# Taking a gate increment out of SP's stream in three gather passes of a four-layer graph network

## The reference

```
# layer 0: messages from source rows and 3 edge features, summed at the destination
tmp = relu(concat(h[src], edge_attr) @ W1.T + b1)
hN  = segment_sum(tmp, dst);  y = relu(concat(h, hN) @ W2.T);  x += y / norm(y)
# layer 1: eight relations
xt  = einsum('ni,rio->rno', h, weight)
x  += relu(segment_sum(xt[edge_type, dst], src) + bias)
# layer 2: attention with 8 heads, softmax over the edges of a destination, batch norm
# layer 3: gcn
x  += leaky(segment_sum(w[:, None] * h[dst], src) @ W + b)
```

## Time and profile before

| what | value |
|---|---|
| median of three runs | 7142.75 us |
| the three runs | 7142.75, 7143.59, 7132.6 us |
| profiled execution, span of the page | 7126.6 us |
| profiled execution, another time than the span | none on the page |
| busy in the span | PE 60%, POOL 54%, DVE 47%, PEld 38%, ACT 20% |
| DMA | 541.25 MB, mean 76 GB/s |
| mean granted clock of PE | 0.676 of full speed |

### The profile page before, as it was taken

The page is one execution under the profiler, slowest core; times in us unless marked ns, Lnnn a source line. Parts: engine busy times, 40 slices in busy tenths (PEclk is TensorE's granted clock), DMA queues, the critical chain, the costliest instruction groups (busy, mean ns, idle before and its releaser), DMA issues. The chain is left out here.

```text
span 7126.6 us, 113087 instructions
## 1 busy us (share of the span) xinstructions
PE 4263.3 (60%) x13279; PEld 2710.9 (38%) x13284; DVE 3340.4 (47%) x11588; ACT 1440.5 (20%) x4442; POOL 3826.6 (54%) x4006
## 2 busy tenths in 40 slices
PE   4324666667724434966665665777777764656665
PEld 1202333333313211434343334555566553434443
DVE  5124555666502101345555555555555564444444
ACT  0202333333312100100000002444444440000000
POOL 3465555555562574036666665555555525666665
PEclk7655766666656656976667676777766766776677
DMA  1112333333300101434444443333333324444443
GB/s 45 40 30 58 80 80 81 80 78 78 73 6 1 32 21 49 147 107 98 98 98 97 97 98 77 82 80 82 82 81 81 81 62 94 95 94 95 94 94 87
DMA packets 1059254, 541.25 MB, mean 76 GB/s; under 512 B 864525, under 2 KB 956238, under 8 KB 1058889
## 3 DMA queue, kind: packets, MB, share of 16 engines
q0 software_dynamic: 177920, 424.21, 21.2%
q1 hardware_dynamic: 507624, 90.64, 6.8%
q10 hardware_dynamic: 373600, 25.30, 3.3%
HBM read 449.78 MB, written 89.82 MB: 76 GB/s over the span
## 5 line engine op out<-in xcount | busy, mean ns | idle before, releaser
L1727 PE MATMUL psS_plain_src<-got_plain_src,hot_plain_src 128*128 x3328 | 1374.7, 561 | 982.0 <-SPq L1558 559.6
L1727 PEld LDWEIGHTS psS_plain_src<-got_plain_src,hot_plain_src 128*128 128x128 f32 x3328 | 828.0, 273 | 1477.6 <-issue 1356.1
L685 POOL DMA_INDIRECT got_attend_dst<-dram_gtab,recs_attend_dst x832 | 812.2, 976 | 643.3 <-DVE msg_attend_dst L766 300.1
L1601 DVE TENSOR_TENSOR sums<-sums,psS_plain_src 128x257 f32 x1664 | 700.8, 421 | 901.6 <-issue 412.4
L1576 POOL DMA_INDIRECT got_edge_mlp_dst<-dram_ptab,rows_i_edge_mlp_dst x784 | 741.8, 946 | 595.4 <-SPq L1555 402.1
L561 POOL DMA_INDIRECT dram_rec_src<-rec_src x784 | 765.7, 977 | 508.3 <-issue 245.4
L1576 POOL DMA_INDIRECT got_plain_src<-dram_xtab,rows_i_plain_src x784 | 746.7, 952 | 478.3 <-SPq L1555 292.1
L1576 POOL DMA_INDIRECT got_plain_src<-dram_htab,rows_i_plain_src x784 | 746.7, 952 | 456.0 <-SPq L1555 268.6
L1738 PE MATMUL psS_edge_mlp_dst<-msg_edge_mlp_dst,hot_edge_mlp_dst 128*128 128x256 f32 x1664 | 792.2, 607 | 173.2 <-DVE sage_sums L1601 89.0
L880 PE MATMUL psS_attend_dst<-msg_attend_dst,hot_attend_dst 128*128 128x264 f32 x1664 | 757.2, 549 | 41.1 <-issue 32.0
L1948 PE MATMUL psO_tab<-w_tab,hT_tab 128*128 128x512 f32 (+1 forms) x980 | 476.8, 636 | 348.7 <-DVE out_tab L1924 190.9
(11 more groups left out here) (366 smaller groups left out, 4563.9 us busy)
## 6 DMA issues: line engine op xcount, KB each, us to landing
dram_xtab<-out_tab SPq DMA_DIRECT2D x48, 1024.0 KB
recs_plain_src<-dram_rec_src ACTq DMA_DIRECT2D x1664, 4.0 KB
recs_edge_mlp_dst<-dram_rec_dst ACTq DMA_DIRECT2D x832, 4.0 KB
recs_attend_dst<-dram_rec_dst SPq DMA_DIRECT2D x832, 4.0 KB
got_attend_dst<-dram_gtab,recs_attend_dst POOLq DMA_INDIRECT x832
dram_rec_src<-rec_src POOLq DMA_INDIRECT x784
got_edge_mlp_dst<-dram_ptab,rows_i_edge_mlp_dst POOLq DMA_INDIRECT x784
got_plain_src<-dram_xtab,rows_i_plain_src POOLq DMA_INDIRECT x784
```

The lines of the kernel that those rows point to most:

```text
L685: nc.gpsimd.indirect_dma_start(got[:, u, 0:w], None, table, bass.IndirectOffsetOnAxis(rec_i[:, u, index_word:index_word + 1], 0)).then_inc ...
L1601: nc.vector.tensor_tensor(here, here, psS[t[1] % banks][:, 0:cols], ALU.add).then_inc(added, 1)
L1727: nc.tensor.matmul(psS[t[1] % banks][:, 0:cols], hot[:, t[1], :], flat[:, bass.ds(slots.of(u), cols)], start=True, stop=True).then_inc(sum ...
```

## The change

The two lines of the gate go out of SP's program in `pair_pass`: its construction, and the step between the wait for used pairs and the raise of `free`. Other gates of the kernel, on SP in `edge_pass`, on DVE and on POOL, stay.

```diff
         @block.sync
         def _(sp):
-            gate = Gate(sp, c.passed["sp"])
             pairs_of = Places(nc.sync, (done, 0), tiles, U, sh.NT, least=1)
...
                     sp.wait_ge(used, pairs_of.of(u))
-                    gate.step()
                     sp.sem_inc(free, 1)
                 if (t := tiles.at(i, u, AHEAD)) is not None:
                     sp.wait_ge(row_in[t[1]], 16 * (t[0] + 1))
                     sp.sem_inc(landed, 1)
```

## The result

The kernel became slower: 7168.27 us (median of 8 runs, 7160.27 to 7185.72) against 7142.86 (8 runs, 7132.6 to 7159.09), a ratio of 1.0041 with a 95% interval of 1.0031 to 1.0051. The 25 us are on the other side of "no change" from the forecast of 150 us gained, and the time lies above the range.

A forecast was written before the change was run, and what follows sets the result against it. SP's instruction stream was taken to bound passes B and C. Gains of 142 us there and 8 us in pass A made 150 us, from the 7142.75 us median to 6993 us; range 6880 to 7150.

The forecast's parts named there:

- no change: Rival, chance 0.09: SP keeps four instructions a tile, or 0.71 us pieces come by the clock; time 7143 us.
- In B and C SP's instruction stream itself is what sets the pace: Plain passes on dram_xtab (B) and dram_htab (C): SP waits for practically nothing, yet POOL waits for SP.
- 221 to 243 us of waiting for L1555: POOL's real waiting before gathers, 243 us in pass B and 221 in C, nearly all for SP's raise of free.
- The price: What one removed SP instruction saves: 0.067 us at the fast pace, 0.61 us at the slow one.
- a count of 13 pieces for 16 instructions: Slow stretch of pass C: 16 SP instructions in 9.8 us, so fewer instructions should need fewer 0.71 us pieces.
- The cycle: Passes B and C: SP crawls during gathers, sprints when POOL lacks slots; one instruction less means fewer pauses.
- The 189 us: Gain in passes B and C from fewer POOL pauses: 99 us in B and 90 us in C.
- the 142 taken: Three quarters of the 189 us gain in passes B and C; the quarter off was a choice.
- Small gain: Rival, chance 0.20: SP relieved, but PE or ACT's record loads take over; gain 20 to 100 us, time 7043 to 7123.
- Pass A: The edge_mlp pass, 612 to 1947 us: only the step from used to free gets shorter, gain 8 us.
- if the cover fails (ACT made slower by closer gathers), pass A loses: Rival "slower", chance 0.15: closer gathers in the edge_mlp pass shrink ACT's good time; time about 7205 us.
- 65 us as the price: Slower rival's loss in the edge_mlp pass: 10% more of ACT's 651 us of unexplained idle.

The follow-up runs named there:

- e3: Kernel before with a second gate increment behind the first in all three passes; ratio 0.9952, 7016.34 us against 7049.93.
- e2: Kernel before with the gate taken out of pass A alone; ratio 1.0030, pass A 1339.0 us.
- e1: Kernel before with the gate taken out of passes B and C, kept in pass A; ratio 1.0014, pass A 1327.1 us.
- e12: Separate small program: 160 semaphore increments on SP, alone, beside 24 POOL gathers, beside ACT loads and more; 0.24 us an instruction beside gathers.
- e14: Kernel before, pass A without the gate, POOL blanking a small tile and waiting for it ahead of each gather; ratio 1.0018, pass A 1353.8 us.
- e10: Kernel before with three gates in pass A, ahead of the wait for used; B and C keep one; ratio 0.9890, 6973.47 us.
- e8: Kernel before with three gates in pass A, between the wait for used and the raise of free; ratio 0.9891, pass A 1268.3 us.
- e11: Kernel before, pass A without the gate but with three more SP register instructions a tile ahead of the wait; ratio 0.9883, 6973.64 us.
- e4: Kernel before with its one gate moved behind the raise of free; ratio 1.0015, pass A 1330.6 us.
- e9: Kernel before without the gate in any of the three passes, one more SP register record a tile ahead of the wait; ratio 1.0018.
- e13: Kernel before, pass A without SP's gate but with three increments per pair on PE's queue; ratio 1.0060, pass A 1370.5 us.
- e15: Kernel before with five gates in pass A, ahead of the wait for used; ratio 0.9934, pass A 1291.6 us.
- e5: Kernel before, gate kept, DVE adding only 32 of 257 columns in pass C; ratio 0.9987, pass C 1205.6 us.
- e6: Kernel before without the gate in any pass, DVE adding only 32 of 257 columns in pass C; ratio 1.0043, pass C 1196.4 us.

## Why the prediction was wrong

The step that failed is "In B and C SP's instruction stream itself is what sets the pace". It rested on SP's absent waits together with POOL's 221 to 243 us of waiting for L1555. Two gates in B and C should then have cost about as much as one was to give; they cost 28 us in both against one (e3 against e2) and 16 against none at all (e3 against e1), and taking one away made B 6 us longer and C 6 us shorter. The instruction did have a price on SP: the 313.5 us of new wait over 1536 instructions are an estimate of 0.20 us each. The passes gave none of it back. The reading that fits is that SP was nearly always late by about as much as used was late. A queue that is held up for 0.71 us at a time, and then comes to a wait already met, shows no wait, whether or not the wait would have lasted as long: absence of waits showed that SP had no slack, not that its slack was worth anything. After the change the 313.5 us of wait appeared at once.

**The price.** The two paces of SP, 0.067 and 0.61 us, are real (e12: 0.061 alone, 0.61 in the last 18 us beside gathers), but they belong to the stretch, not to the instruction. The pieces are time in which the instruction streams of SP, DVE, ACT and PE hardly get on. The rival "no change" had named just that, "the pieces of 0.71 us come by the clock and not by the instruction", and I dismissed it on a count of 13 pieces for 16 instructions. The count was short: the stretch holds 19 records of SP's four lines (5, 5, 4 and 5), 0.52 us each and not 0.61. And in e12 the same instruction goes by five to ten and by one to three between two hold-ups in one run, so such a count belongs to the stretch and can't tell whether fewer instructions need fewer pieces.

**The cycle.** "SP crawls while gathers follow one another, POOL eats up the free slots, stops, SP sprints" may describe the rows rightly, but with 1536 fewer instructions POOL's waiting in B and C didn't shrink (484.4 and 450.2 us of idle against 478.3 and 456.0), so a shorter sprint is not what ends POOL's pause. The 189 us from it and the 142 taken were gains on a link that was not the last; they should have been nothing.

**Small gain.** Its mechanism happened (SP's wait for used over 100 us, PE's waiting passed on to DVE), but it ended at no gain in B and C: the next link was level with SP. That PE, DVE and ACT had room by their busy time did not help, as their streams can be held up beside gathers too (e12); before, PE stood 652.2 us ahead of its weight loads with nothing named.

**Pass A.** I took 8 us of gain and got 25 of loss (21 by e2's ratio). The reason given there for a loss, "if the cover fails (ACT made slower by closer gathers), pass A loses", had the right place and the right sign, but not the right way. Of 65 us as the price it was 25, and its condition isn't borne out: spacing the gathers without SP (e14) gave back some 10 us, the instructions on SP up to 90 (e10 against e2: 1339.0 to 1246.0). ACT's idle without a reason changed little (275.7 + 226.6 + 156.9 = 659 us against 651 before); PE's wait for DVE's adds grew instead, from 84.0 to 180.8 us.

**The skill.** By the rule of the Trainium skill's "Perfetto Trace Analysis", section Identifying the Most-Contended Engine, SP was not worth an edit and the sum 0; that is nearer to the result than my 142 us, but it gives neither the loss nor the 1.1% that other edits of SP's stream were worth (e8, e10, e11). "Trainium Architecture — The Big Picture" of the Trainium skill, section What this means for kernel authors, calls the engines independent processors. For their instruction streams beside gathers the measurement disagrees: SP's increments take 0.24 us beside POOL's gathers and 0.061 alone, with no semaphore between the two.

**What is shown and what is open.** Shown: the larger part of the loss is A's (e1, e2); it is due to missing instructions in SP's stream, of whatever kind and on whichever side of the wait for used (e4, e8 to e11), and as many and more on PE's do not make up for them (e13); more of them make A shorter up to three, and longer at five (e15, at a lower clock); in C DVE's arithmetic has no part (e5, e6). What goes with a short pass A is that DVE and ACT have fewer pieces of 0.71 us: 241 and 654 after the change, 190 and 625 before, 72 and 512 with three gates (e8). A fitting reading is that a slower SP raises free and landed evenly, so that DVE and ACT run into fewer held stretches, while an SP with slack answers each used at once and in bunches. That reading is argued, not shown, and three rows stand against its simplest form: e14 has 156 and 623 pieces, fewer than before, in an A of 1353.8 us, and in pass C the change took DVE and ACT from 173 and 611 to 406 and 739 with C no longer for it. And e3 has the fewest of all kernels in C, 69 and 393, with C 16 us longer than in e2 (189 and 615). No run holds the bunches apart from SP's pace, and the order of single events can't be read in held stretches, where the records bunch. So by what way three instructions on SP shorten the loop of A stays open.

## What to carry to other kernels

A queue without waits has no slack; that doesn't make it the bound. Double its suspected cost before you remove it: e3 would have told in one run that SP's instructions in B and C were worth 5 to 18 ns each and that in A they were worth less than nothing. In a loop of several engines around an indirect gather, one instruction more or less in the feeding queue is worth a sweep of three or four values, per pass: here three in A gave 1.1%, and two more in the attention pass cost nearly 100 us.

## What the runs showed of the hardware

Indirect gathers issued on POOL hold up the control instructions of SP, ACT, DVE and PE at the same times, in pieces of about 0.71 us: 28 whole ones on SP beside 24 gathers when it counts alone, 41 to 47 on each engine when all four do; small loads of ACT's queue do not (e12: 160 increments of 17 ns each). With gathers 1.25 us apart an increment of SP takes 0.13 us on average in the first 12 us and 0.61 us behind that. An instruction without any purpose can pay: three increments of a semaphore that nobody waits for, in a pass of 784 tiles, shortened it from 1333 to 1268 us. And the records in such stretches bunch, several starts within 20 ns of each other where unhindered ones are 57 ns apart, so that short waits of a queue can't be read from them.
